# Eight more TensorE products of constants behind the sums of 28 of 32 scan units

## What is computed

```python
dbc = einsum('bse,re->bsr', u, Wdbc)             # 64 + 16 + 16 columns
dlt, Bm, Cm = split(dbc, [R, R + N], axis=-1)
delta = softplus(einsum('bsr,er->bse', dlt, Wdt) + bdt)
dA = exp(delta[..., None] * A)                   # (b, s, 512, 16)
dBu = delta[..., None] * Bm[:, :, None, :] * u[..., None]
def step(h, xs):
    dA_t, dBu_t, C_t = xs
    h = dA_t * h + dBu_t
    return h, einsum('ben,bn->be', h, C_t)       # the sum over 16 states
```

## Time and profile before

| | |
|---|---|
| median of 3 runs | 5706.89 us (5706.18 to 5708.85) |
| profiled execution, its own time | 5708.02 us |
| its span | 5706.3 us |
| mean granted clock of TensorE | 0.773 |
| VectorE (DVE) busy | 4861.3 us, 85% of the span |
| TensorE (PE) busy | 4166.5 us, 73%, 24,852 products |
| ScalarE (ACT) busy | 3695.1 us, 65% |
| GpSimd (POOL) busy | 3172.3 us, 56% |
| chain that ended last | DVE 43%, PE 38%, issue 7%, POOL 4%, ACT 4% |
| DMA | 578.96 MB, mean 101 GB/s |

### The profile page before, as it was taken

The page is one execution under the profiler, slowest core; times in us unless marked ns, Lnnn a source line. Parts: engine busy times, 40 slices in busy tenths (PEclk is TensorE's granted clock), DMA queues, the critical chain, the costliest instruction groups (busy, mean ns, idle before and its releaser), DMA issues.

```text
span 5706.3 us, 69820 instructions
## 1 busy us (share of the span) xinstructions
PE 4166.5 (73%) x24852; PEld 2571.2 (45%) x24852; DVE 4861.3 (85%) x4908; ACT 3695.1 (65%) x8614; POOL 3172.3 (56%) x1452
## 2 busy tenths in 40 slices
PE   5667777778777777787777777777777777777644
PEld 4444444445444444444444444444444444444322
DVE  4228899998999989999999898999998998899896
ACT  0136676766667767666677666767766676677653
POOL 0015566656566655566666556666665566666564
PEclk7667777777878878778787778878877788778766
DMA  3013444443344444434444444344444434444441
GB/s 94 3 45 97 103 117 111 105 113 94 103 102 116 109 111 110 114 92 107 107 116 109 105 113 99 102 102 112 110 114 106 114 95 105 107 116 109 103 117 47
DMA packets 348556, 578.96 MB, mean 101 GB/s; under 512 B 58497, under 2 KB 151818, under 8 KB 340014
## 3 DMA queue, kind: packets, MB, share of 16 engines
q1 hardware_dynamic: 348206, 574.51, 39.7%
HBM read 436.93 MB, written 136.92 MB: 101 GB/s over the span
## 4 chain that ended last, share of the span: by engine, by line
DVE 43%; PE 38%; issue 7%; POOL 4%; ACT 4%; DVEq 0%; DMA 0%; SPq 0%; POOLq 0%; ACTq 0%
DVE S_X L714 20%; PE ps L164 20%; DVE ps L706 11%; PE ps L750 5%; PE ps L386 4%; PE ps L365 4%; POOL S_X L736 3%; DVE A_sm L422 2%; PE ps L154 2%; DVE A_raw L129 1%; PE ps L395 1%; ACT A_ring L147 1%; ACT A_ring L463 1%; PE ps L521 1%; DVE C_wa L562 1%
## 5 line engine op out<-in xcount | busy, mean ns | idle before, releaser
L736 POOL TENSOR_TENSOR S_X<-S_X,S_bc 128x1024 f32<-128x1024 f32 x1024 | 2411.9, 2355 | 1830.3 <-DVE ps L706 1830.1
L714 DVE TENSOR_TENSOR_SCAN S_X<-S_dA,ps 128x1024 f32<-128x1024 f32 x1024 | 2338.9, 2284 | 99.7 <-PE ps L750 5.9
L686 ACT ACTIVATE S_dA<-S_slot,acol 128x255 f32<-128x255 f32 x4096 | 1720.1, 497 | 628.2 <-DVE S_X L714 625.4
L706 DVE TENSOR_TENSOR ps<-S_slot,S_bc 128x1024 f32<-128x1024 f32 x1024 | 1311.9, 1281 | 27.0 <-DVE S_X L714 0.9
L750 PE MATMUL ps<-S_X,sum 128*32 128x256 f32 x8192 | 793.7, 493 | 641.0 <-POOL S_X L736 614.7
L750 PEld LDWEIGHTS ps<-S_X,sum 128*32 128x32 f32 x8192 | 219.0, 126 | 1024.5 <-POOL S_X L736 749.5
L365 PE MATMUL ps<-A_kP,A_qP 32*128 32x256 f32 x2048 | 394.9, 517 | 123.7 <-DVE A_sm L422 123.6
L154 PE MATMUL ps<-ident,A_ring 128*128 128x128 f32 x768 | 156.8, 339 | 401.8 <-ACT A_ring L147 302.1
L422 DVE TENSOR_REDUCE A_sm<-ps 128x4 f32<-128x1024 f32 x256 | 312.0, 1219 | 133.1 <-PE ps L365 133.0
L386 PE MATMUL ps<-A_qP,A_kP 32*128 32x256 f32 x2048 | 354.5, 472 | 64.8 <-ACT A_ring L463 53.2
L463 ACT ACTIVATE A_ring<-ps 128x1024 f32<-128x1024 f32 x256 | 260.6, 1018 | 179.3 <-PE ps L386 179.3
(11 more groups left out here) (312 smaller groups left out, 7270.8 us busy)
## 6 DMA issues: line engine op xcount, KB each, us to landing
S_slot<-scr_dd SPq DMA_DIRECT2D x1024, 256.0 KB, 4.9
scr_dd<-C_dd SPq DMA_DIRECT2D x64, 1024.0 KB, 4.8
S_bc<-scr_bc SPq DMA_DIRECT2D x256, 256.0 KB, 5.4
scr_wa<-C_wa SPq DMA_DIRECT2D x32, 1024.0 KB, 7.5
S_wa<-scr_wa SPq DMA_DIRECT2D x32, 1024.0 KB, 8.7
C_mod<-scr_mod SPq DMA_DIRECT2D x32, 512.0 KB, 9.5
scr_g<-S_g SPq DMA_DIRECT2D x32, 512.0 KB, 6.7
T_g<-scr_g SPq DMA_DIRECT2D x32, 512.0 KB
```

The source lines that it names most:

```text
L686: ins = a.activation(B["dA"][:, s, q % 2, j, lo:lo + T - 1], B["slot"][:, s, j, 0, lo:lo + T - 1], ACT.Exp, scale=K.k["acol"][:, s, 4 * c ...
L706: v.tensor_tensor(B["in"], B["slot"][:, s, :, 1, :], rep(B["bc"][:, s, q, :], 1, 4), ALU.mult).then_inc(S.dve.sem, 1)
L714: v.tensor_tensor_scan(line(X[:, u % 4]), line(B["dA"][:, s, q % 2]), line(B["in"]), 0.0, ALU.mult, ALU.add).then_inc(S.dve.sem, 1)
L736: g.tensor_tensor(B["X"][:, u % 4], B["X"][:, u % 4], rep(B["bc"][:, s, NQ + q, :], 1, 4), ALU.mult).then_inc(S.pool.sem, 1)
```

## The change

Behind the four products of each unit that isn't the last of its block, and behind their signal, eight more products of the same form are issued: the same fixed operand `sum4`, the same four quarters of the output partitions, 256 columns each. Their moving operand is a weight of L0 in place of the scan's result, and they accumulate into the half of bank 5 that the block does not use. These values are read by nobody: the first unit of the next block starts its sum anew. No wait and no signal is added.

```diff
         ins.then_inc(S.pe.sem, 1)
+        if not last:
+
+            for n in range(2):
+                for j in range(4):
+                    p.matmul(B["bank"][32 * j:32 * j + 32, (1 - c % 2) * T:(2 - c % 2) * T], K.k["sum4"][:], K.k["L0wq"][:, n, :],
+                             start=False, stop=False, tile_position=(0, 32 * j), skip_group_check=True)
```

## The result

| | before | after |
|---|---|---|
| median | 5707.87 us (4 runs, 5706.18 to 5708.93) | 5979.91 us (4 runs, 5973.45 to 5985.72) |
| profiled execution, its own time | 5708.02 | 5973.45 |
| its span | 5706.3 | 5971.7 |
| mean granted clock | 0.773 | 0.86 |
| PE busy, records of products (two for each float32 product) | 4166.5, 24,852 | 4653.8, 39,188 |

The ratio is 1.0477 [1.0458, 1.0495], so the change costs 272 us. The forecast was 5851 with a range of 5640 to 5990: right in sign and within the range, but short by half of the amount, and just outside the narrower range of its main case (5760 to 5970).

What follows compares the result with a forecast made beforehand. VectorE's own work bounds the kernel (91% busy), with stretches of waiting for TensorE between. Costs at places on the path less the clock's gains sum to +4.5 us a turn, times 32 batches +144: 5851 us, range 5640 to 5990.

Steps and rivals of the forecast that it cites:

- main case: Whole kernel: slower by two to three per cent, 5760 to 5970 us; chance 0.65.
- two output projections (T_x, A_x): L3 and L1 projections that VectorE waits for: three fillers ahead, partly at half clock, add +3.0 us a turn.
- copy of K: Product that VectorE copies, behind four units: their fillers delay it, +2.1 us a turn averaged over two turns.
- L212: Product whose statistics VectorE takes, behind two units: 0.3 us of slack, fillers make it later, +1.2 us a turn.
- behind it, the L0 projection: Projection ending just before VectorE turns to it: one more filler in its chain, +0.5 us a turn.
- wf (C_xh): Product with wf, 6.50 us at half clock, 3.72 at full: clock up before it, VectorE's wait goes, -1.3 a turn.
- S_g: VectorE wait, 1.1 us a turn, in a half-clock stretch with units among it: raised clock takes it down by 0.7.
- T_qm: VectorE wait in the same half-clock stretch as S_g: raised clock takes it down by 0.3 us a turn.
- Where the clock gives back: Half-clock stretches with dense fillers: raised clock shortens the waits for wf (-1.3), S_g (-0.7) and T_qm (-0.3) a turn.
- By the chain: Cross-check on the chain of waits: 9.7 filler groups cost 10.5 us, faster TensorE returns 5.5: +5.0 us a turn.
- The clock that stays up throughout: Rival: all of the chain's TensorE work at full clock, -5.1 us a turn, 5544 us; chance 0.22, mostly at 5600 to 5690.
- The unchanged clock: Rival: added products don't lift the clock, +381 us, 6088 us; chance 0.07.

Runs made afterwards that it cites:

- e1: Changed kernel without the fillers behind nine units (3, 4, 8 to 11, 28 to 30), leaving those behind 19: 5779.26 us, ratio 1.0115.
- e8: Changed kernel plus one more group of eight products behind unit 15, just ahead of the scores and wf: 5889.74 us, ratio 1.0318.
- e7: Changed kernel with two full products (128 rows, identity as fixed operand) in place of each filler's eight: 5931.04 us, ratio 1.0395.
- e6: Changed kernel without the fillers behind units 21 and 22: 6075.21 us, ratio 1.0643.
- e5: Changed kernel with two full-width products over 32 rows in place of each filler's eight: 6524.72 us, ratio 1.1429.
- e3: Changed kernel with filler products for one quarter of the output partitions only, two in place of eight: 5980.77 us, ratio 1.0476.
- e2: Changed kernel with fillers only behind units 3, 4, 8 to 11 and 28 to 30: 5821.18 us, ratio 1.0195.
- p2: Kernel before plus five groups in TensorE's idle time ahead of L1's output projection and one behind unit 27: 5690.85 us, ratio 0.9964.

## Why the prediction was right in sign and short by half

Terms of the sum against what VectorE waited more, per turn:

| step | predicted | measured |
|---|---|---|
| two output projections (T_x, A_x) | +3.0 | +2.5 |
| copy of K | +2.1 | +3.2 |
| L212 | +1.2 | +1.6 |
| behind it, the L0 projection | +0.5 | +0.7, at another place |
| wf (C_xh) | -1.3 | +0.6 |
| S_g | -0.7 | +1.0 |
| T_qm | -0.3 | +0.4 |
| A_sm | 0 | 0 |
| sum, and all waits | +4.5 | +10.0 |

That the total came out at half and not less is in part luck. The prediction multiplied by 32 batches, but the growth of 9.5 us a turn came in the 28.6 turns of the steady stretch (9.5 x 28.6 = 272). With 28.6 its +4.5 would have been +129 and not +144. Small slips beside that: 3.4 less 1.7 at the copy of K is 1.7, not 1.6, and the 6.50 us read for wf are its longest, for it took 4.9 to 6.5.

**The costs** were found at their places and were nearly right. Of the projections, A_x's +0.8 is one filler at full clock, the 0.86 of the prediction. For the copy of K the wait grew from 0.65 to 3.8 a turn, 3.2, close to four fillers at full clock (3.4). The 1.7 of gain that I granted the first turn for a raised clock didn't come: TensorE is idle ahead for 3.52 us (2.67 in the turn that I had read), and the first of the four fillers runs at half clock behind it. The L0 projection has no VectorE wait of note; a wait of 0.7 came on ScalarE's exponentials instead, a sign of the kind that by the prediction's own words makes its terms wrong even with the total right. It comes from the stretch of L212, through ScalarE's waits for transposes and projections. The size for L212 was near, but its cause is only partly the fillers' time: e1 has the wait without them.

**The step that failed is "Where the clock gives back"**: -2.3 predicted, +2.0 measured, 4.3 of the 5.5 us by which the sum was short. (The turn grew by 9.5, for VectorE's own work is 0.5 less.) That fillers raise the clock was right, and the cold share fell to 26%, the value chosen. Some of that match is luck, for one of the two stretches that it counted on, that of wf, stayed cold in part. What was wrong is the place. I took it that dense fillers in a stretch raise the clock for all that follows in it, and credited the gain to wf and to the end of the block. But the one unit of a block that has no filler, `last`, stands right ahead of the scores and wf, with idle time behind it, and there the clock falls: wf took 6.1 us or more in every turn of the steady stretch. e8 shows that one group in that place brings the gain, though e7 has it without. For S_g it is another matter: the fillers of units 21 and 22 stand in front of the sum that it waits for, and its wait falls by 1.2 a turn without them (e6). The diff said which units have no filler. The prediction listed it only for bank 5's safety and never asked what stands behind those four units.

**By the chain** the estimate was +5.0, with 9.7 groups on the chain. The chain after has L757 at 9.7% of 4974 us in the steady stretch, 482 us or 16.9 a turn, against the 10.5 that I gave it: some 16 groups at the same price each (an estimate). The fillers put themselves on the path, as VectorE waits more often and more groups lie in front of something it waits for. Here the count of units on the chain of before was too low for the groups on the chain after.

**The rivals.** The clock that stays up throughout did not come, for idle time of 6.5 us stayed, as argued. The unchanged clock, 6088, is excluded by 0.86; e5 shows a price for it, 6525, well above the 6088. Cost in the number of instructions, which I had set at zero, doesn't show in e3 either.

What stays open is why the effects of e1 and e2 don't add, in numbers, and what sets the steps of a turn. The traces show that a clock change moves when fillers elsewhere come or go (L212 in e1, all of e6, wf in e7), but I can't work out from rows where it will fall.

## What to carry to other kernels

Products that only keep the clock up have to be priced place by place: ahead of a product that another engine already waits for they can cost nearly their full time (the copy of K, 3.2 us for four that take 3.4), elsewhere much less (3.8 us of the whole time for each place in e1, against 12.6 in e2), and in idle time ahead of the path nothing in all (p2). 16 to 18 groups, half of them or more in idle time or behind unit 15 and the rest where a filler had cost no wait, won 1.9 to 2.0% where 28 placed by rule lost 4.8%. Look first at which places the rule leaves out and what runs behind those; then read the granted clock over the whole turn after each step, because a filler taken or added can move the places where it falls. And look at the length of a turn itself: if it comes in steps, small differences between variants say little about the price of one product.

## What the hardware showed that was not expected

- With fillers for one quarter of the output partitions TensorE was busy as long, and clock and time were the same, as with four quarters (0.858 and 5980.77 us against 0.86 and 5979.91).
- With fillers of 32 rows the clock was 0.776, with fillers of 128 rows 0.884, and the times lie 594 us apart, at equal length of a filler at full clock (1.12 and 1.13 us). TensorE was busy for 9.00 us of 9.00 at 0.50.
- The turns lock into a pattern: in the changed kernel the wait for the copy of K came in 27 turns at 4.05 us on average and 4.2 at most, in e6 the turns were of one length, 177.5 us, and in the changed kernel and in e1 to e8 eight turns took lengths that are whole steps of 13.7 us apart. Taking out two fillers (e6) made the kernel 95 us slower.
